# Causal attention of a two-layer decoder: when the next group's four projections are asked, 2+2 against 1+2+1

## The reference

```
q  = x @ wq.T                         # 16 heads of 64
kv = x @ w_kv_down.T                  # latent, 128 wide
k, v = kv @ w_k_up.T, kv @ w_v_up.T   # 16 heads of 64
q, k = q*cos + rotate_half(q)*sin, k*cos + rotate_half(k)*sin
p  = softmax(q @ k.T / 8 + causal)
x  = layernorm(x + (p @ v) @ wo.T)
```

## Time and profile before

| | before |
|---|---|
| median of the runs | 3760.81 us |
| profiled execution, own time | 3774.66 us |
| its span | 3772.9 us |
| PE busy in the span | 3239.7 us (86%) |
| DVE / ACT / POOL busy | 2021.9 / 1912.6 / 971.6 us |
| mean granted TensorE clock | 0.943 |

### The profile page before, as it was taken

The page is one execution under the profiler, slowest core; times in us unless marked ns, Lnnn a source line. Parts: engine busy times, 40 slices in busy tenths (PEclk is TensorE's granted clock), DMA queues, the critical chain, the costliest instruction groups (busy, mean ns, idle before and its releaser), DMA issues. The chain is left out here.

```text
span 3772.9 us, 75675 instructions
## 1 busy us (share of the span) xinstructions
PE 3239.7 (86%) x26784; PEld 2516.2 (67%) x26784; DVE 2021.9 (54%) x6791; ACT 1912.6 (51%) x4678; POOL 971.6 (26%) x790
## 2 busy tenths in 40 slices
PE   7888888869799589998899878999999948999970
PEld 4666566558688366666666665777777737999960
DVE  5777777768677355554555444466666750000016
ACT  6878788745522265555655545655555621222210
POOL 0000000027200576667677720001111130000014
PEclk9999999989899799999999998999999978999995
DMA  6111011100100222222222211000000035555543
GB/s 197 57 44 58 33 52 52 62 6 1 65 1 1 75 59 52 52 55 54 54 54 58 52 29 58 14 13 18 21 25 25 24 130 173 182 182 182 182 136 113
DMA packets 128784, 254.79 MB, mean 68 GB/s; under 512 B 24928, under 2 KB 67360, under 8 KB 123552
## 3 DMA queue, kind: packets, MB, share of 16 engines
q1 hardware_dynamic: 117520, 198.55, 17.5%
q0 software_dynamic: 10896, 51.39, 3.6%
HBM read 159.03 MB, written 57.28 MB: 57 GB/s over the span
## 5 line engine op out<-in xcount | busy, mean ns | idle before, releaser
L988 PE MATMUL a_T<-ident,a_t 128*128 128x128 f32 x3328 | 500.3, 284 | 89.6 <-ACT a_pT L1158 63.3
L988 PEld LDWEIGHTS a_T<-ident,a_t 128*128 128x128 f32 x3328 | 375.5, 144 | 284.5 <-issue 249.9
L1158 ACT ACTIVATE a_pT<-a_T 128x512 f32<-128x512 f32 (+3 forms) x768 | 368.6, 511 | 225.5 <-PE a_T L988 225.4
L1401 DVE CUSTOM_DVE_ANT_0 a_t<-a_A,a_decay 128x512 f32<-128x512 f32 x512 | 323.0, 687 | 101.8 <-PE a_A L953 101.6
L1171 ACT ACTIVATE a_t<-a_t,a_neg 128x512 f32<-128x512 f32 x512 | 362.6, 716 | 5.8 <-DVE a_neg L1412 4.5
L1406 DVE CUSTOM_DVE_ANT_0 a_t<-a_A,a_table 128x384 f32<-128x384 f32 (+3 forms) x512 | 221.1, 487 | 175.4 <-PE a_A L965 174.5
L1232 POOL TENSOR_TENSOR a_rsin<-a_rawswapped,a_sin 128x512 f32<-128x512 f32 x128 | 170.4, 1331 | 513.2 <-DMA a_rawswapped<-a_raw 425.9
L2453 DVE COPY experts_y<-experts_Y 128x256 f32<-128x256 f32 x72 | 30.6, 425 | 497.3 <-PE experts_Y L2394 497.3
L2435 ACT ACTIVATE experts_hT<-experts_H 128x512 f32<-128x512 f32 x144 | 86.0, 597 | 414.9 <-PE experts_H L2408 414.9
L1171 ACT ACTIVATE a_t<-a_t,a_mx 128x384 f32<-128x384 f32 (+3 forms) x512 | 280.0, 551 | 0.0
L2408 PEld LDWEIGHTS experts_H<-experts_xgT,experts_w 128*128 128x128 f32 x2304 | 270.3, 193 | 8.7 <-issue 4.1
(11 more groups left out here) (334 smaller groups left out, 6684.1 us busy)
## 6 DMA issues: line engine op xcount, KB each, us to landing
experts_w<-in_f_w_dram SPq DMA_DIRECT2D x72, 1024.0 KB, 5.0
moe_sent<-a_zeros POOLq DMA_DIRECT2D x33, 1024.0 KB, 8.4
a_rawswapped<-a_raw SPq DMA_DIRECT2D x512, 64.0 KB, 2.0
a_invrep<-a_inv_dram SPq DMA_DIRECT2D x64, 256.0 KB, 4.0
experts_xg<-moe_sent SPq DMA_DIRECT2D x72, 128.0 KB, 2.0
moe_results<-experts_y SPq DMA_DIRECT2D x72, 128.0 KB, 1.8
x_invrep<-x_inv_dram SPq DMA_DIRECT2D x32, 256.0 KB, 3.9
ex_w<-in_f_w_dram SPq DMA_DIRECT2D x8, 1024.0 KB
```

Of the source, the lines that this page charges most:

```text
L988: mm = pe.transpose(bank[:, kt, :], t_of(u, j, kt * P, (kt + 1) * P), sh.ident[:])
L1158: nc.scalar.activation(to, of, ACT.Copy).then_inc(t_empty, 1)
L1401: nc.vector.tensor_tensor_reduce(t_of(s, j, 0, n), A[seg.bank(name)][:, 0:n], table[:, at:at + n], 1.0, LOWEST, ALU.mult, ALU.max, mx[:, s ...
```

## The change

Within a batch the four items of the next group are no longer asked two and two in steps 0 and 1, but one, two and one in steps 0, 1 and 2. Group 3, which asks for the next batch's items, keeps two and two. It is one line of `tasks`:

```diff
         if g + 1 < G:
-            items = {"a0": ([0], [1], [], []), "a1": ([0, 1], [2, 3], [], []), "x1": ([0, 1], [2, 3], [4], [])}[kind]
+            items = {"a0": ([0], [1], [], []), "a1": ([0], [1, 2], [3], []), "x1": ([0, 1], [2, 3], [4], [])}[kind]
             works = [("item", g + 1, i) for i in items[at]]
```

## The result

The change takes 3733.93 us (median of 4 runs, 3726.83 to 3738.56), the kernel before 3762.94 us in the runs beside it (4 runs, 3760.76 to 3766.59): ratio 0.9915, 95% interval 0.9901 to 0.9929, or 29 us less. The profiled execution of the change has a span of 3734.4 us and an own time of 3736.23. All medians in this text leave out slow executions; there was one, of the experiment with two copies (3835.95 us, at a mean granted clock of 0.879).

What follows compares the result with a forecast made beforehand. PE was taken to bound causal attention, so reordering could only win or lose its idle time. A gain of 14.4 us at group ends less 1.0 gave 13.4 us, forecast 3747.4 us, range 3737 to 3763.

Steps and rivals of the forecast that it cites:

- The chain: Group ends: item 3's swap delays spill, spread, `oT`, step 3's scores and PE's next first bank; spill 1.31 us earlier.
- about 4: Sign at group ends: PE's waits at L924 and L834 for DVE fall from 24.1 us together to about 4.
- 11 x 1.31: Ends of groups in causal attention: 11 of 14 each gain the spill's 1.31 us, 14.4 us in all.
- PE's lateness: PE reaches step 3 later by 0.35 us, 0.6 in group 0; free while the wait at the group's end covers it.
- `oT` waits for PE in groups 0 and 2: Sign that the forecast is wrong: at these groups' ends `oT` waits for PE; no size given.
- the margin of 2.9 us: Group 1: POOL ends item 3 3.4 us later than before, still 2.9 us before PE wants it for scores.
- No wait of L965 for POOL beyond those of before: Sign at the first scores: no new PE waits for POOL; such waits in many groups would show the forecast wrong.
- a share of 1.0: 1.0 us deducted for uncovered lateness in batches 4 and 7, group 2, and for POOL close behind in batch 0.
- PE late too: Rival at group ends: PE's lateness eats the gain, each end some 0.3 us, 0 to -7 us; chance 0.24.
- POOL becomes the gate, slower: Rival: item 3's swap lands late, next group's first scores wait for POOL; slower, up to +13 us; chance 0.10.
- More than the sum: Upper variant: ACT keeps up in steps 1 and 2, 20 to 24 us gained; chance 0.66 together with the forecast.

Runs made afterwards that it cites:

- e1: Kernel before, items in the old order; only SyncE's queue issues item 3's swap behind the spread, in groups 0 to 2: 3733.59 us, ratio 0.9931.
- e2: The change's order of items, but SyncE's queue issues item 3's swap ahead of spill and spread again: 3761.9 us, ratio 1.0001 to the kernel before.
- e7: Kernel before with old queue and item order, but four buffers instead of two for `rawswapped`: 3726.35 us, ratio 0.9911.
- e10: The change itself, unaltered, timed once more beside the kernel before: 3732.71 us, ratio 0.9915.
- e12: The change itself again, on one chip beside a repeat of the kernel before with four `rawswapped` buffers: 3734.10 us, ratio 0.9919 to the kernel before.
- e8: The change with three extra copies of an output bank on DVE ahead of `oT`, ends of groups 0 and 2: 3772.59 us, ratio 1.003 to the kernel before.
- e3: Kernel before, items in the old order, with item 3's swap issued behind the spread in all four groups: 3731.18 us, ratio 0.9915.
- e5: The change with two extra copies of an output bank on DVE ahead of `oT`, ends of groups 0 and 2: 3753.27 us, ratio 0.998 to the kernel before.

## Why the prediction was wrong in size and right in its mechanism

**The chain holds.** Item 3's swap, spill, spread, `oT`, scores, first bank: each link was seen to move, and e1, e2 and e7 put the whole gain on the first. The forecast that the spill is left 0.07 us behind `turned` in place of 1.38 came out to the hundredth in the group read, and L924 and L834 fell to 4.2 us where "about 4" was forecast.

**The term that failed: 14.4 us, "11 x 1.31".** The step behind it is the prediction's sentence that "a change of order can only win or lose PE's idle time": it prices an end by the length of its wait and takes PE's busy time as given. Measured, busy time fell by 11.7 us in the first profile (11.2 in the means), priced at nothing. 12.9 us of long runs of L924 and L844 stood behind the old waits in the profile of before and none in that of the change; L860's runs took 3.9 us more, 1 of them for two matmuls more in the stretch. The long runs could be read before: one line showed 5.38 beside 3.69 us for the same 16 matmuls. Removing the wait of 1.71 in the earlier trace rows removed 3.54 - 1.88 = 1.66 us behind it.

The idle part of the term was too small as well. The two waits lost 24.1 - 4.2 = 19.9 us and not 14.4. In the group read, counted from item 0's L858, `oT` came 1.73 us earlier (23.38 to 21.65) and not 1.31: `turned` came 0.15 and the spread's issue behind the spill another 0.20 earlier. The net idle time fell by 12.1 us in the first profile, because (among smaller changes) 6.9 us went to waits for POOL and 1.7 to group 3's wait at L858, and by 17.0 in the means. That 12.1 lies close to the forecast's 13.4 is luck: terms that were too small on both sides met.

**PE's lateness.** New idle time in step 1 was 0.60 us for the 0.75 forecast, and step 2's wait of 0.40 is gone. The sum came out under the 0.35 forecast: from item 0's L858 until PE was ready for L834 it took 1595.90 - 1.71 - 1570.57 = 23.62 us before and 1589.05 - 1565.44 = 23.61 now. Waits of L988 for ACT didn't rise in sum (25.8 to 24.9 us).

**`oT` waits for PE in groups 0 and 2,** which the forecast called a sign of error. It does so at 10 of the 15 ends, against 2 before, by 1.24 us in the group read: the spread came earlier than the 1.31 reckoned. It means that at these ends the spread no longer holds anything, not that the chain was wrong; the sign was badly chosen.

**POOL.** In group 1 item 3 waited 3.19 us for its swap (3.4 later was forecast) and ended at 1565.49 + 1.27 = 1566.76, 1.6 us ahead of the first scores at 1568.38: the margin of 2.9 us was 1.3 too large. In group 2 it ended at 1594.90, again 1.6 ahead of the scores, where 3.9 was forecast. In the sum the rival took a part: first scores wait 6.9 us more for POOL (21.6 to 28.5; 31.0 and 30.4 in e10 and e12). "No wait of L965 for POOL beyond those of before" was wrong. 5.1 us of it are in batch 0, groups 1 and 2 (6.02 and 1.81 us for 2.69 and none), for which the forecast had set aside a share of 1.0; in the other batches such waits stay under 0.8 us in the change's three profiles, but for the stretch's last one, which reaches 2.0. By e2 the items bring them, with the swap ahead of the spill. `rsum` may be part of it, which no run separates: the waits before POOL's second operation, L1236, for it rose from 3.4 us in 3 waits to 13.0 in 15, of which 12 stand in this line of POOL's waits:

```profile
POOL a_khl L1236 <- DVE a_rsum L1290: 9.1, 12, 1.2
```

By the rule of the Trainium skill (SBUF — State Buffer, Who interferes with whom) a DVE instruction with two SBUF inputs contends with a GpSimd instruction that reads SBUF. The rows agree: the moved `rsum` took 1.04 us beside POOL where two took 1.29 beside an idle one.

**The rivals.** "PE late too" and "POOL becomes the gate, slower" didn't happen. "More than the sum" named 20 to 24 us and the wrong reason, ACT; idle time alone gave 12 to 17 us, and the matmuls' shorter time the rest.

## What to carry to other kernels

Price a wait on the matmul engine by its length and by the duration of the matmuls behind it: list the same line's runs, and where some are longer than others, read the granted clock of that stretch. Look in a queue's order for a transfer that waits on a buffer ahead of one that is already due; giving it a buffer of its own was worth as much here as moving it, and perhaps more. Compare intervals that hold the same instructions: where work has moved past the mark from which one counts, the difference is wrong by its length. Name as a sign of error only what would contradict the mechanism.

## What was not expected of the hardware

Behind waits of 1.67 to 3.21 us PE often ran 16 matmuls of 256 columns in 5.38 us instead of 3.69, at a mean granted clock of 0.68. It is not each such wait: L924's runs stayed at 3.69 us behind 1.75 and 1.76 us in e8, 1.98 in e3, 2.04 in e2 and 2.06 in e7. None read was long behind a wait of 1.57 or less. L844, which comes after a second wait of 0.69 us for ACT, was long in e5 behind first waits of 1.08, 1.19 and 1.42 us, and not behind one of 1.78. So the length of the wait alone doesn't tell; what else does is open. A delay of `oT` costs more than its length: 38.7 us for 26.5 us of work. And one profiled execution had a last stage of 118.6 us where the thirteen others had 101.7 to 102.2, the change's among them with the same number of instructions; its cause isn't known.
